# First pass of a two-layer graph network kernel: group comparisons and their sums moved forward, filler matmuls in the first turns, one group check moved ahead of the gathers

## The chip, the cores and the metric

The kernel runs on one core of one Trainium2 chip. The metric is the device time of one execution in microseconds (us). The median of three runs before the change is 1245.95 us. Engines are named as the profile names them: PE (TensorE; PEld is its weight load), DVE (VectorE), ACT (ScalarE), POOL (GpSimd) and SP (SyncE, which only issues DMAs here).

## The reference

Two graph layers run over 100000 nodes with 64 features and 50000 edges, and the edges come sorted by `dst` but not by `src`. Cut to what matters:

```python
h = maximum(layernorm(x), 0)                       # unused by layer 0 but for its shape
s   = segment_sum(edge_attr, src, N)               # layer 0: sum, max, mean of 32 edge features per src node
mx  = where(cnt > 0, segment_max(edge_attr, src, N), 0)
x   = x + relu(concat([s, mx, s / maximum(cnt, 1), u]) @ W1 + b1) @ W2 + b2
h   = maximum(layernorm(x), 0)                     # layer 1
x   = x + relu(segment_sum(h[src], dst, N) @ W.T + b)
```

## The kernel before

The edges are cut into 98 blocks of 512, the nodes into 98 blocks of 1024 rows (8 groups of 128 nodes).

- **Sort (0 to about 171 us).** DVE sorts the edges by `src` in SBUF with compare and exchange steps (lines L931 to L959). Most of them are `tensor_tensor` operations with both inputs in SBUF. Between them PE turns the tile over. `beside_turn` and `between_turns` put other small work between the steps.
- **First pass (from about 186 us).** POOL gathers the edge features of a block into one of eight buffers `xa` with four indirect DMAs (L543). DVE scales them (`scale_attr`, L1073), PE turns them (`turn_attr`), DVE runs two scans over them (`scans`, L1085 and L1087), PE multiplies by W1 (`layer1`), ACT takes the relu (`hidden`, L696), PE multiplies by W2 (`layer2`, L1372), and DVE subtracts a constant row (`less_constant`, L1135) into a record that ACT stores to DRAM. Four to seven turns later windows of records are read back (SP and ACT issue the loads), DVE builds one-hot matrices (`onehots`, L1108), PE expands the records to node rows with them (`expand`, L1384) and DVE adds x (`add_dense`, L1127). In turn n every engine works through its own fixed list: DVE does `scans(n)`, `add_dense(n-7)`, `keys_to_psum(n-5)`, `scale_attr(n+2)`, `onehots(n-5)`, `less_constant(n-1)`. PE does `turn_attr(n+1)`, `expand(n-6)`, `layer2(n-1)`, `layer1(n)`. ACT does `hidden(n-1)`, a record's key and store, then its share of the window loads.
- **Where the windows start.** To load a window the kernel must know at which record each group of 128 nodes begins. `rows_above` compares 800 group numbers with 12 bounds (twelve DVE operations on 128 x 800 f16, L844) and takes the number of edges in each group (L846, L847). `sum_starts` adds these up over the partitions with 24 matmuls of 400 columns (L1309). ACT copies the sums, and `group_starts` on DVE (L852) turns them into `start_row`, for which SP and ACT wait before the first window load (`s_start`). The same is done for `dst` during the sort, where ACT made the comparisons; the result is `near_f`.
- **Checks.** After its last gather of the first pass, POOL checks for `src` and then for `dst` whether the groups fit into the windows (L578 to L587, each operation on one partition with 800 or 784 elements), and presets two one-hot buffers (L573). These share the memory of `above`. ACT sums the checks, and `choice` on DVE (L859) picks the fast path.
- **Second pass (from 713 us).** POOL gathers node rows from the table that the first pass wrote (L562), and a like pipeline runs for `dst`.

In PE's list of the first pass `stream` (L1389) is a matmul of ones whose result nobody reads; `expand` starts with one.

Of the kernel before, what the change touches and what calls it, by code (L numbers as in the profile page):

```python
# [15 lines left out]
P = 128  # L16
# [9 lines left out]
BT = 4  # L26
BLK = BT * P
BLOCKS = -(-E // BLK)
PAIRS = BLOCKS // 2
STEP = 1024  # L30
UNIT = 128
# [38 lines left out]
def valid(n):  # L70

    return 0 <= n < BLOCKS


def build(nc, x, src, dst, edge_attr, u, W1, b1, W2, b2, W, b, src_keys, dst_keys, src_cols, dst_cols, dst_lines, out):
# [5 lines left out]
    with ExitStack() as ctx:  # L81
# [407 lines left out]
        def _(pool):  # L489
# [75 lines left out]

            pool.wait_ge(s_gi, 1)
            for n in range(BLOCKS):
                gather_attr(n)
            for b_ in range(XRING):
                pool.wait_ge(gathered[b_], 16 * BT * len(range(b_, BLOCKS, XRING)))  # L570
            pool.wait_ge(s_base, 2)
            for r, t in enumerate(hot1):
                g.tensor_copy(t[96:P, :, :], ident[96:P, CONST[1]:CONST[1] + 1].unsqueeze(2).to_broadcast([P - 96, PER, UNIT])).then_inc(s_preset1, 1)  # L573
                pool.wait_ge(s_preset1, r + 1)
            pool.wait_ge(s_near, 2)
            pool.wait_ge(s_cast, 2)
            for side, (row, more) in enumerate(((start_f, over), (near_f, over2))):
                link(g.tensor_scalar(room[:, :], row[:, :], float(-ROW), None, ALU.mult))  # L578
                link(g.tensor_tensor(room[:, :], room[:, :], limit[:, :], ALU.add))
                link(g.tensor_scalar(more[:, :], room[:, :], 0.0, None, ALU.is_lt))  # L580
                if side == 1:
                    link(g.tensor_scalar(room[:, :], room[:, :], 0.0, None, ALU.max))
                    link(g.tensor_tensor(room[:, :], limit[:, :], room[:, :], ALU.subtract))
                    link(g.tensor_copy(start_row[1][:, :], room[:, :]))
                link(g.tensor_tensor(room[:, 0:LAST], row[:, 1:LAST + 1], row[:, 0:LAST], ALU.subtract))
                link(g.tensor_scalar(room[:, 0:LAST], room[:, 0:LAST], float(WP), None, ALU.is_gt))
                last = g.tensor_tensor(more[:, 0:LAST], more[:, 0:LAST], room[:, 0:LAST], ALU.add)  # L587
                if side == 0:
                    link(last)
            last.then_inc(s_over, 1)  # L590
            pool.wait_ge(s_fast, 1)
# [36 lines left out]
        def _(act):  # L628
# [30 lines left out]

            act.wait_ge(s_base, 1)  # L660
            for h, row in enumerate(p_s[1]):
# [66 lines left out]
            for n in range(BLOCKS + SRC_WIN):  # L728
# [4 lines left out]
                if n == 3:  # L733
                    act.wait_ge(s_base, 2)
                    for h, row in enumerate(p_s[0]):
                        last = s.copy(start_f[:, 400 * h:400 * (h + 1)], row[0:1, 0:400])
                    last.then_inc(s_near, 1)
# [45 lines left out]
        def _(dve):  # L783
# [56 lines left out]

            def rows_above():

                for k in range(SPAN):
                    v.tensor_scalar(above[:, k, :], group_of[:, :], bound_u[:, k:k + 1], None, ALU.is_gt)  # L844
                dve.wait_ge(s_signs, SPAN * 2)
                link(v.tensor_scalar(less[:, 1:SPAN + 1], signs[:, :], 0.5, COLS / 2, ALU.mult, ALU.add))  # L846
                v.tensor_tensor(in_group[:, :], less[:, 1:SPAN + 1], less[:, 0:SPAN], ALU.subtract).then_inc(s_above, 1)  # L847
# [292 lines left out]
            scale_attr(0)  # L1140
            scale_attr(1)
            for n in range(BLOCKS + SRC_ADD):
                if valid(n):
                    scans(n)
                if valid(n - SRC_ADD):
                    add_dense(0, n - SRC_ADD)
                if valid(n - SRC_HOT):
                    keys_to_psum(0, n - SRC_HOT)
                if valid(n + 2):
                    scale_attr(n + 2)  # L1150
                if valid(n - SRC_HOT):
                    onehots(0, n - SRC_HOT)
                if valid(n - SRC_REC):
                    less_constant(n - SRC_REC)
                if n == 1:
                    rows_above()
                if n == 3:
                    group_starts()
# [129 lines left out]
        def _(pe):  # L1288
# [14 lines left out]

            def sum_starts(side, nth):

                pe.wait_ge(s_above, nth)
                for h, row in enumerate(p_s[side]):
                    for k in range(SPAN):
                        last = mm(row[0:1, 0:400], in_group[:, k:k + 1], above[:, k, 400 * h:400 * (h + 1)],  # L1309
                                  start=k == 0, stop=k == SPAN - 1)  # L1310
                last.then_inc(s_base, 1)
# [10 lines left out]
            def between_turns(t):  # L1322

                if t == 7:
                    sum_starts(1, 1)
                elif t == 5:
# [19 lines left out]
            pe.wait_ge(s_tt[0], 19)  # L1346
            turn_columns(p_u, ha).then_inc(s_pt[0], 1)
            pe.wait_ge(s_tt[0], 20)
            pe.wait_ge(s_gi, 1)
# [42 lines left out]
            for n in range(BLOCKS + SRC_EXP):  # L1392
                if valid(n + 1):
                    turn_attr(n + 1)
                if n == 2:
                    sum_starts(0, 2)
                if valid(n - SRC_EXP):
# [98 lines left out]
```

## Time and profile before

| | us |
|---|---|
| three runs | 1242.65, 1245.95, 1247.1 (median 1245.95) |
| the profiled execution, own time | 1242.97 |
| its span | 1241.2 |
| busy DVE, PE, POOL, ACT | 1021.4, 957.0, 786.6, 282.4 |
| first scan of the first pass | 189.08 |
| last addition of the first pass ends | 709.9 |
| first gather of the second pass | 713.01 |

A row of a timeline gives the start (us), the duration (us), engine, line, operation, output and inputs, shapes, the count of merged instructions, and in brackets how long the engine had been idle before it and what ended that. Times are from the span's start.

### The profile page before, as it was taken

How to read it: one execution, taken by the hardware profiler on the slowest of the kernel's cores; microseconds unless marked ns; L12 is line 12 of the kernel's file. 1: busy time of each engine (PE TensorE's matmuls, PEld its weight loads, DVE VectorE, ACT ScalarE, POOL GpSimd, SP SyncE). 2: the span in 40 equal slices, each digit the busy share in tenths (PEclk: the TensorE clock that was granted, in tenths of full speed). 3: DMA queues.
4: the chain of work that ended last, by engine and by line, in shares of the span. 5: the costliest groups of instructions: out<-in, count | busy, mean ns of one | idle time of the engine just before them, and what ended most of it. 6: DMA issues, size and time to landing. Idle time of an engine off the chain costs nothing.

```text
span 1241.2 us, 20776 instructions
## 1 busy us (share of the span) xinstructions
PE 957.0 (77%) x5818; PEld 758.3 (61%) x5818; DVE 1021.4 (82%) x2718; ACT 282.4 (23%) x685; POOL 786.6 (63%) x836
## 2 busy tenths in 40 slices
PE   0122017999999999999999725898888888978988
PEld 0011004777777777777777514776777677766777
DVE  8888896899999999999999635777677777777785
ACT  1451032222222222222222111111121212111110
POOL 3000037777777777777777577777777777777750
PEclk9996556799999999999999955888898989898989
DMA  2000012788989888888888645686887778787865
GB/s 66 0 0 0 0 32 71 169 229 240 236 232 239 234 234 235 225 231 221 232 228 234 185 136 125 168 230 175 229 211 202 207 197 211 205 221 203 214 172 161
DMA packets 317579, 218.51 MB, mean 176 GB/s; under 512 B 223444, under 2 KB 255156, under 8 KB 317460
## 3 DMA queue, kind: packets, MB, share of 16 engines
q1 hardware_dynamic: 182116, 135.41, 38.8%
q10 hardware_dynamic: 110256, 62.42, 19.3%
q0 software_dynamic: 25088, 19.32, 8.1%
q8 instruction: 47, 0.77, 0.3%
q14 instruction: 72, 0.59, 0.2%
HBM read 137.51 MB, written 79.45 MB: 175 GB/s over the span
## 4 chain that ended last, share of the span: by engine, by line
DVE 48%; POOL 13%; DMA 12%; PE 10%; issue 8%; ACTq 5%; ACT 2%; SPq 0%; DVEq 0%; POOLq 0%
POOL xa L562 13%; DMA xa<-node_table,gi 8%; DVE feats L1087 8%; DVE feats L1085 7%; DVE oneh L1108 6%; DVE dout L1127 4%; DMA win<-records 3%; ACTq L686 3%; DVE rec L1135 2%; DVE kb L933 2%; DVE ka L933 2%; PE p_m L1372 2%; DVE shared L1108 2%; ACT hid L696 2%; DVE ka L934 2%
## 5 line engine op out<-in xcount | busy, mean ns | idle before, releaser
L543 POOL DMA_INDIRECT xa<-in_edge_attr_dram,gi x392 | 374.2, 955 | 232.3 <-issue 119.0
L562 POOL DMA_INDIRECT xa<-node_table,gi x392 | 370.9, 946 | 131.9 <-issue 108.0
L696 ACT ACTIVATE hid<-p_z,bias_z 128x512 f32<-128x512 f32 x98 | 113.7, 1160 | 236.1 <-issue 222.8
L1087 DVE TENSOR_TENSOR_SCAN feats<-c_rows,feats,p_g 32x512 f32<-32x512 f32 x97 | 123.3, 1271 | 1.4
L1413 PE MATMUL p_g<-ident,hn 128*128 128x128 f32 x196 | 46.3, 324 | 100.5 <-DVE hn L1187 100.4
L1085 DVE TENSOR_TENSOR_SCAN feats<-c_rows,feats,p_g 64x512 f32<-64x512 f32 x97 | 122.5, 1263 | 0.5 <-issue 0.5
L749 ACT ACTIVATE sd<-mv,eps_t 128x4 f32<-128x4 f32 x98 | 29.2, 298 | 399.2 <-DVE mv L1178 342.9
L1108 DVE SCALAR_TENSOR_TENSOR oneh<-p_m,node_of 112x1024 f32<-112x1024 f32 x98 | 119.3, 1218 | 0.2
L1372 PE MATMUL p_m<-w_s,hid 128*128 128x64 f32 x784 | 109.2, 283 | 13.0 <-ACT hid L696 12.5
L1108 DVE SCALAR_TENSOR_TENSOR shared<-p_m,node_of 112x1024 f32<-112x1024 f32 x98 | 117.3, 1197 | 2.2 <-PE p_z L1384 0.6
L1389 PE MATMUL p_t<-one 128*128 128x256 f32 (+1 forms) x228 | 113.3, 582 | 0.0
L1384 PEld LDWEIGHTS p_u<-win,oneh 128*128 128x128 f32 x784 | 95.8, 193 | 26.9 <-issue 22.5
L1389 PE MATMUL p_u<-one 128*128 128x512 f32 x230 | 111.2, 568 | 0.0
L1384 PEld LDWEIGHTS p_t<-win,oneh 128*128 128x128 f32 x784 | 95.9, 193 | 24.1 <-issue 23.5
L1365 PE MATMUL p_z<-feats,w_s 96*128 96x512 f32 x196 | 109.4, 640 | 0.4 <-DVE feats L1087 0.4
L1372 PEld LDWEIGHTS p_m<-w_s,hid 128*128 128x128 f32 x784 | 97.4, 195 | 18.7 <-ACT hid L696 16.7
L1173 DVE BATCH_NORM_STATS2 stat<-xa 128x6 f32<-128x64 f32 x392 | 58.7, 212 | 59.9 <-DMA xa<-node_table,gi 59.8
L1098 DVE COPY p_m<-win 112x8 f32<-112x8 f32 x196 | 32.9, 168 | 79.8 <-DMA win<-records 79.7
L1384 PE MATMUL p_u<-win,oneh 128*128 128x64 f32 x784 | 93.8, 273 | 2.8 <-DVE oneh L1108 2.8
L1384 PE MATMUL p_t<-win,oneh 128*128 128x64 f32 x784 | 93.5, 273 | 0.0
L1413 PEld LDWEIGHTS p_g<-ident,hn 128*128 128x128 f32 x196 | 25.4, 159 | 110.0 <-DVE hn L1187 109.7
L1187 DVE SCALAR_TENSOR_TENSOR hn<-xa,mv,p_m 128x64 f32<-128x64 f32 x392 | 83.9, 277 | 3.5
(259 smaller groups left out, 1565.7 us busy)
## 6 DMA issues: line engine op xcount, KB each, us to landing
win<-records SPq DMA_DIRECT2D x980, 28.9 KB
records<-rec ACTq DMA_DIRECT2D x196, 132.0 KB
din<-in_x_dram SPq DMA_DIRECT2D x49, 512.0 KB
node_table<-dout SPq DMA_DIRECT2D x48, 512.0 KB, 3.9
din<-node_table SPq DMA_DIRECT2D x43, 512.0 KB
out_dram<-dout SPq DMA_DIRECT2D x43, 512.0 KB
c_rows<-rows_src ACTq DMA_DIRECT2D x141, 128.0 KB
win<-records ACTq DMA_DIRECT2D x588, 28.9 KB
```

What stands on the lines that cost most here:

```text
L543: g.indirect_dma_start(out=xa[n % XRING][:, t, 0:FE], out_offset=None, in_=edge_attr, in_offset=bass.IndirectOffsetOnAxis(ap=gi[0][:, BT * ...
L562: g.indirect_dma_start(out=xa[k % XRING][:, t, :], out_offset=None, in_=T, in_offset=bass.IndirectOffsetOnAxis(ap=gi[1][:, BT * n + t:BT * ...
L696: s.activation(hid[n % 2][:, :].rearrange("p (t n) -> p n t", n=P), p_z[n % 2][:, :].rearrange("p (n t) -> p n t", t=BT), ACT.Relu, bias=b ...
L1085: v.tensor_tensor_scan(f[0:64, :], c[0:64, at:at + BLK], p_g[n % 2][0:64, :], first[0:64], ALU.mult, ALU.add)
L1087: v.tensor_tensor_scan(f[64:96, :], c[64:96, at:at + BLK], p_g[n % 2][0:32, :], first[64:96], ALU.min, ALU.max).then_inc(feats_ok, 1)
L1108: v.scalar_tensor_tensor(hots[side][m % HRING][0:WP, :, :], key_at(k).unsqueeze(2).to_broadcast([WP, PER, UNIT]), -float(STEP * m), node_o ...
L1187: last = v.scalar_tensor_tensor(hn[n % 2][:, t, :], xa[(BLOCKS + n) % XRING][:, t, :], mv[n % 2][:, t, 0:1], up[:, t:t + 1].to_broadcast([ ...
L1365: mm(p_z[n % 2][:, :], w1_s[:, :], feats[n % 2][:, :], start=True, stop=True).then_inc(z_ok, 1)
L1372: last = mm(p_m[0][:, D * t:D * (t + 1)], hid[n % 2][:, P * t:P * (t + 1)], w2_s[:, :], start=True, stop=True)
L1384: last = mm(to[:, D * s:D * (s + 1)], hots[side][m % HRING][:, s, :], win[k % WRING][:, s, 0:D], start=True, stop=True)
L1389: mm(bank[:, 0:width], one[:, :], one[:, :].unsqueeze(1).to_broadcast([P, width // P, P]), start=True, stop=True)
L1413: last = tr(p_g[n % 2][:, P * h:P * (h + 1)], hn[n % 2][:, 2 * h:2 * h + 2, :].rearrange("p t d -> p (t d)"), ident[:, :])
```

## The change

Four edits, all in the first pass and the sort:

1. `rows_above` is split. The first six comparisons stand ahead of turn 0, the other six and the group counts (`rows_in_group`) in turn 0, behind `scale_attr(2)` and ahead of the second scan. Before, all of it stood in turn 1.
2. `sum_starts` works on one half (12 matmuls). For `src` the halves stand in turns 1 and 2 of PE's list, before `layer2`; before, both stood in turn 2. For `dst` both halves still stand at the same place of the sort.
3. Filler matmuls of ones: two into the two `p_z` banks between the turn of `ha` and the turns of `sorted_in` and `spare`, and a `stream` into `p_z` in each of turns 0, 3, 4 and 5.
4. POOL checks the `dst` groups once `near_f` is there, ahead of the first gather of the first pass. Only the check for `src` stays behind the last gather, and the presets of `hot1` come behind that.

```diff
-            for side, (row, more) in enumerate(((start_f, over), (near_f, over2))):
+            def check_groups(side, row, more):
...
+            pool.wait_ge(s_near, 1)
+            pool.wait_ge(s_cast, 2)
+            check_groups(1, near_f, over2)
             pool.wait_ge(s_gi, 1)
             for n in range(BLOCKS):
                 gather_attr(n)
             for b_ in range(XRING):
                 pool.wait_ge(gathered[b_], 16 * BT * len(range(b_, BLOCKS, XRING)))
-            pool.wait_ge(s_base, 2)
-            for r, t in enumerate(hot1):
...
+            pool.wait_ge(s_near, 2)
+            check_groups(0, start_f, over)
+            pool.wait_ge(s_base, 4)
+            for r, t in enumerate(hot1):
...
-                    act.wait_ge(s_base, 2)
+                    act.wait_ge(s_base, 4)
...
             scale_attr(1)
+            rows_above(0, SPAN // 2)
             for n in range(BLOCKS + SRC_ADD):
...
                     onehots(0, n - SRC_HOT)
+                if n == 0:
+                    rows_above(SPAN // 2, SPAN)
+                    rows_in_group()
                 if valid(n - SRC_REC):
                     less_constant(n - SRC_REC)
-                if n == 1:
-                    rows_above()
...
+            def sum_starts(side, h):
+
+                pe.wait_ge(s_above, 2 - side)
+                for k in range(SPAN):
+                    last = mm(p_s[side][h][0:1, 0:400], in_group[:, k:k + 1], above[:, k, 400 * h:400 * (h + 1)],
+                              start=k == 0, stop=k == SPAN - 1)
                 last.then_inc(s_base, 1)
...
                 if t == 7:
+                    sum_starts(1, 0)
                     sum_starts(1, 1)
...
             turn_columns(p_u, ha).then_inc(s_pt[0], 1)
+            for z in p_z:
+                mm(z[:, :], one[:, :], one[:, :].unsqueeze(1).to_broadcast([P, BT, P]), start=True, stop=True)
...
-                if n == 2:
-                    sum_starts(0, 2)
+                if n in (1, 2):
+                    sum_starts(0, n - 1)
+                elif n < SRC_EXP:
+                    stream(p_z[n % 2], BLK)
```

## Rows read from the trace of the kernel before

**Rows 1.** The page: shares of the chain that ended last.

```profile
DVE 48%; POOL 13%; DMA 12%; PE 10%; issue 8%; ACTq 5%; ACT 2%; SPq 0%; DVEq 0%; POOLq 0%
```

**Rows 2.** Timeline of DVE in the first turns.

```profile
189.08 1.27 DVE L1085 TENSOR_TENSOR_SCAN feats<-c_rows,carry,p_g 64x512 f32<-64x512 f32 x1 [2.34 <-PE p_g L1360]
...
197.05 0.42 DVE L1135 TENSOR_TENSOR rec<-p_m,c_neg 128x256 f32<-128x256 f32 x1 [2.30 <-PE p_m L1372]
197.39 4.25 DVE L844 TENSOR_SCALAR shared<-group_of,bound_u 128x800 f16<-128x800 f16 x12
...
209.11 0.43 DVE L1135 TENSOR_TENSOR rec<-p_m,c_neg 128x256 f32<-128x256 f32 x1 [4.37 <-PE p_m L1372]
...
212.70 0.97 DVE L852 SCALAR_TENSOR_TENSOR start_row<-start_f,limit 1x800 int32<-1x800 f32 x1
```

**Rows 3.** Waits, 184 to 240 us: us in total, times, longest.

```profile
DVE rec L1135 <- PE p_m L1372: 12.8, 5, 4.4
```

**Rows 4.** Timeline of PE in the first turns.

```profile
186.20 1.13 PE L1301 MATMUL p_t<-ident,ka 128*128 128x128 f32 x4 [2.50 <-DVE ka L1051]
...
201.98 4.03 PE L1309 MATMUL p_t<-shared,in_group 128*1 128x400 f16 x12 [2.30 <-DVE in_group L847]
205.84 2.19 PE L1309 MATMUL p_u<-shared,in_group 128*1 128x400 f16 x12
...
222.23 1.97 PE L1372 MATMUL p_m<-w_s,hid 128*128 128x64 f32 x8 [0.93 <-ACT hid L696]
...
226.66 1.91 PE L1389 MATMUL p_t<-one 128*128 128x512 f32 x2
...
235.55 1.06 PE L1372 MATMUL p_m<-w_s,hid 128*128 128x64 f32 x8
```

**Rows 5.** Busy times by stretch; PEclk is the granted clock.

```profile
200.00:205.00 5.00, 3.02 (x10) 1.18 (x11) 4.66 (x10) 0.03 (x1) 3.99 (x4) 0.50 0.32 85
...
220.00:225.00 5.00, 4.07 (x15) 2.78 (x14) 3.91 (x7) 1.33 (x2) 3.78 (x5) 0.50 0.77 199
...
230.00:235.00 5.00, 5.00 (x36) 3.96 (x35) 3.15 (x4) 1.01 (x2) 3.78 (x5) 1.00 0.62 169
```

**Rows 6.** Timelines of POOL and DVE: a middle block's and the last block's gathers.

```profile
473.00 0.95 POOL L543 DMA_INDIRECT xa<-in_edge_attr_dram,gi  x1 [0.31 <-issue]
...
482.37 0.28 DVE L1073 TENSOR_TENSOR xa<-xa,share 128x128 f32<-128x128 f32 x1
...
663.55 0.95 POOL L543 DMA_INDIRECT xa<-in_edge_attr_dram,gi  x1 [0.30 <-issue]
668.56 2.13 POOL L573 COPY shared<-ident 32x1024 f32<-32x1024 f32 x2 [4.07 <-issue]
```

**Rows 7.** The chain: start, us, what; a gather's way from issue to landing.

```profile
726.89 2.42 DMA xa<-node_table,gi
```

**Rows 8.** Timelines of ACT and POOL around the new place of the check.

```profile
95.62 0.87 ACT L662 COPY near_f<-p_m 1x400 f32<-1x400 f32 x2 [17.16 <-PE p_m L1309]
...
170.97 1.18 POOL L543 DMA_INDIRECT xa<-in_edge_attr_dram,gi  x1 [112.97 <-ACT gi L716]
```

**Rows 9.** Timeline of POOL: the first and last of nine operations of the check that moves.

```profile
683.10 2.20 POOL L578 TENSOR_SCALAR room<-near_f 1x800 f32<-1x800 f32 x1
...
698.59 1.84 POOL L587 TENSOR_TENSOR over<-over,room 1x784 f32<-1x784 f32 x1
```

**Rows 10.** Timelines of POOL and DVE where both read SBUF.

```profile
675.05 2.21 POOL L580 TENSOR_SCALAR over<-room 1x800 f32<-1x800 f32 x1
675.52 0.53 DVE L1073 TENSOR_TENSOR xa<-xa,share 128x128 f32<-128x128 f32 x1
...
212.78 1.72 POOL L543 DMA_INDIRECT xa<-in_edge_attr_dram,gi  x1 [0.30 <-issue]
```

**Rows 11.** Groups of DVE instructions, 96.5 to 113.5 us: busy us, mean ns.

```profile
L933 DVE TENSOR_TENSOR ka<-kb 128x256 f32<-128x256 f32 x8 | 3.4, 426 | 0.3
```

**Rows 12.** Timeline of DVE at the end of the first pass.

```profile
709.85 0.15 DVE L859 TENSOR_REDUCE wrong<-wrong 128x1 f32<-128x6 f32 x1
```

More of the change, by code:

```diff
@@ L564, in gather_x @@
                         in_offset=bass.IndirectOffsetOnAxis(ap=gi[1][:, BT * n + t:BT * n + t + 1], axis=0)).then_inc(gathered[k % XRING], 16)
[L566 to L570, printed above, removed]
-            pool.wait_ge(s_base, 2)
-            for r, t in enumerate(hot1):
[L573 to L576, printed above, removed]
-            for side, (row, more) in enumerate(((start_f, over), (near_f, over2))):
+            def check_groups(side, row, more):
                 link(g.tensor_scalar(room[:, :], row[:, :], float(-ROW), None, ALU.mult))
@@ L587, in _ @@
                 last = g.tensor_tensor(more[:, 0:LAST], more[:, 0:LAST], room[:, 0:LAST], ALU.add)
-                if side == 0:
+                if side == 1:
                     link(last)
-            last.then_inc(s_over, 1)
+                else:
+                    last.then_inc(s_over, 1)
+            pool.wait_ge(s_near, 1)
+            pool.wait_ge(s_cast, 2)
+            check_groups(1, near_f, over2)
+            pool.wait_ge(s_gi, 1)
+            for n in range(BLOCKS):
+                gather_attr(n)
+            for b_ in range(XRING):
+                pool.wait_ge(gathered[b_], 16 * BT * len(range(b_, BLOCKS, XRING)))
+            pool.wait_ge(s_near, 2)
+            check_groups(0, start_f, over)
+            pool.wait_ge(s_base, 4)
+            for r, t in enumerate(hot1):
+                g.tensor_copy(t[96:P, :, :], ident[96:P, CONST[1]:CONST[1] + 1].unsqueeze(2).to_broadcast([P - 96, PER, UNIT])).then_inc(s_preset1, 1)
+                pool.wait_ge(s_preset1, r + 1)
             pool.wait_ge(s_fast, 1)
@@ L658, in _ @@
             act.wait_ge(s_cast, 2)
-            act.wait_ge(s_base, 1)
+            act.wait_ge(s_base, 2)
             for h, row in enumerate(p_s[1]):
@@ L839, in bounds, with rows_above, rows_in_group @@
                 v.tensor_scalar(bound[:, :], bound_u[:, :], float(UNIT), UNIT / 2 - 0.5, ALU.mult, ALU.add).then_inc(s_bound, 1)
-            def rows_above():
-                for k in range(SPAN):
+            def rows_above(first, end):
+                for k in range(first, end):
                     v.tensor_scalar(above[:, k, :], group_of[:, :], bound_u[:, k:k + 1], None, ALU.is_gt)
+            def rows_in_group():
                 dve.wait_ge(s_signs, SPAN * 2)
@@ L1302, in turn_columns @@
                 return last
[L1304 to L1310, printed above, removed]
+            def sum_starts(side, h):
[3 more added lines that the diff above has]
+                              start=k == 0, stop=k == SPAN - 1)
                 last.then_inc(s_base, 1)
```

## Prediction

> **What bounds the kernel now.** I first read the page's shares of the chain that ended last: DVE carries about half of it [rows 1]. Then I read the timelines of DVE, PE, ACT and POOL from 160 to 250 us, turn by turn, since every edit but one lies there. The reader is to see three things. First, a turn from the eighth on is one unbroken row of DVE work, while in turns 1, 2, 4, 5 and 6 DVE waits for PE at `less_constant`; these five waits come to 12.8 us [rows 3], the longest (4.37 us) right behind the sums of `sum_starts`, which hold PE from 201.98 us to 207.97 us [rows 2, 4]. Second, PE runs at the lower of its two levels in most of these turns: the granted clock is 0.50 (1.2 GHz) from 200 to 205 and from 220 to 225 us, after stretches with gaps in PE's work, and 1.00 (2.4 GHz) from 230 us, after turns filled by the stream and the expansion [rows 5]. Third, POOL issues a gather about every 1.25 us without a pause, four to a block, so (663.55 - 473.00) / 38 = 5.01 us a block from block 59 to block 97; DVE scales the same two blocks at 482.37 and 675.52 us, 5.08 us a block with its small stalls [rows 6, 10]. The two go at nearly the same pace. Whatever the first turns give back, DVE then runs closer behind the gathers. After the last block the rest of the pass and the second pass follow at fixed distances.
>
> **The change, part by part.**
>
> *The comparisons.* Twelve take 4.25 us, 0.354 us each [rows 2]. The first six (2.1 us) fall into the 2.34 us in which DVE waits for PE before the first scan [rows 2]: cost nothing; without that cover 2.1 us. The other six and the two small operations for the counts (about 0.3 us) stand ahead of the second scan: it moves from about 191.9 us (two scans and a scaling behind the first) to about 194.4 us. DVE waited 2.30 us at the end of that turn anyway [rows 2], so most of this is hidden too, and 4.5 us leave turn 1.
>
> *The sums.* Twelve matmuls took 4.03 us at the low level and about 2.1 us after the clock rose [rows 4]. The counts are there at about 194.4 us. I take 2.0 us for a half: the first ends at 196.4, `layer2(0)` (1.0 us, [rows 4]) at 197.4, `less_constant(0)` at 197.8: the third scan starts at 197.9 us, where now it stands behind the comparisons and counts (197.39 + 4.25 + 0.2 = 201.9 us, [rows 2]): 4.0 us earlier. The second half ends at about 200.9 and `layer2(1)` at 201.9, where before the record waited until 209.11 us [rows 2]: the fourth scan, right behind the record, starts at 202.3 instead of 209.4 us, 7.1 us earlier. ACT copies the sums at about 204 us, `start_row` follows some 7 us before 212.70 us [rows 2], and so do SP's and ACT's first window loads and everything that ACT has queued behind its wait for them (`hidden(3)` above all).
>
> *The fillers.* Ones of 512 columns take about 1.7 us at the low level (1.91 us is the pair of records, overlapping what follows) and 0.9 us at the high one [rows 4]. Two of them, 3.4 us, go into a gap of 2.50 us before the turns at 186.20 us [rows 4]: up to 0.9 us late, nothing if the clock rises meanwhile. What they are to give is the clock. `layer2` takes 1.97 us at the low level and 1.06 us at the high one [rows 4]. In turns 4 to 6 DVE waits 12.8 - 2.3 - 4.4 = 6.1 us for PE [rows 2, 3]. With a high clock I count 0.9 us less in each of the first two, and 2.5 us in the third, where a stream, an expansion and `layer2` stand in a row: 4.3 us. The eighth scan would start 7.1 + 4.3 = 11.4 us earlier. If the clock gives nothing it is still 7.1 us.
>
> *What the gathers let through.* Here the gain is cut. Block 59's last gather is issued at 473.00 us and its scaling runs at 482.37 us [rows 6], 9.37 us later, the shortest distance from block 5 on that I found. How long a gather takes to land is not shown for these. From below, 2.42 us from issue in a quiet stretch [rows 7]; from above, the last one, issued at 663.55 us, is there by 668.56 us, when POOL comes through its wait for all of them [rows 6]: at most 5.0 us. DMA is busier in this pass than in the quiet stretch, so I take 3.9 us, a little nearer to the upper end. That leaves DVE 9.4 - 3.9 = 5.5 us to gain (4.4 to 6.9). The start-up gain of 7 to 11 us exceeds this, so 5.5 us reach the end of the pass, and DVE shows waits for gathers in their place. The stalls of later turns stay as they are.
>
> *The check that moves.* At its old place it costs nothing: POOL ends at 700.4 us and DVE asks for the verdict at 709.85 us [rows 9, 12], 9.4 us of cover for ACT's two sums, and the check for `src` with the presets behind it is done earlier than both checks were. At its new place POOL is idle until 170.97 us and `near_f` is there at 96.5 us [rows 8], so its nine operations, 17.3 us from first to last [rows 9], never delay the first gather by themselves; the cover is some 57 us. But they read SBUF beside a sort whose every step is on the path. Between 96.5 and 113.5 us DVE has 30 exchange operations with both inputs in SBUF (this group of 8 and three more of 8, 7 and 7) [rows 11]. The trace has one meeting of that kind: with POOL's operation of 675.05 us under way, the scaling of block 97 took 0.53 us instead of 0.28 us [rows 6, 10]. So the price lies between nothing, 9 x 0.25 = 2.3 us (one meeting for each of POOL's operations), 30 x 0.25 = 7.5 us (each exchange is held up) and 17.3 us (DVE stands still while POOL works). The one row shows a delay much shorter than POOL's 2.21 us, so I take 2.3 us and keep 0 and 17.3 as ends. This delay would move the sort's end, the first gather and all that follows.
>
> The Trainium skill, page "SBUF — State Buffer", section "Who interferes with whom", says that a DVE instruction with two SBUF inputs and a GpSimd instruction that reads SBUF share one read interface, and that the later one "fully blocks" until the first has finished. In one direction the trace agrees: a gather issue took 1.72 us instead of 0.95 us beside the DVE operation of 212.70 us, which has two SBUF inputs [rows 2, 10]. In the other it does not: the scaling began 0.47 us into POOL's operation and ended 1.2 us before it did [rows 10]. By the page the change would cost about 17 us less 5.5 us, by my row 2.3 us less 5.5 us.
>
> *Sum.* 2.3 - 5.5 = -3.2 us. The profiled execution's own time is 1242.97 us (1.8 us around the span of 1241.2 us), which gives 1239.8 us. That execution lies 3.0 us below the median of the three runs; the mean of all four is 1244.7 us, and I set the prediction against it: 1241.5 us. A measurement of this kernel can tell about 0.5%, 6.2 us.
>
> **The rivals.**
>
> - *The check is free.* For it: POOL's operations touch a single partition, and the one delayed DVE operation may be chance. Then -5.5 us (-4.4 to -6.9): 1239.2 us.
> - *Each exchange is held up.* 7.5 - 5.5 = +2.0 us: 1246.7 us. For it: the one meeting in the trace did cost 0.25 us. Against: it was one operation after DVE work that has one SBUF input, not a dense row.
> - *DVE stands still while POOL works* (the other side). Place: 96.5 to 114 us, the steps of the sort. Price 17.3 us less the 2.5 us in which DVE waits for PE anyway, so 15 to 17 us: net +9 to +12 us, about 1255 us. It decides from a hold of about 1.3 us for each of the nine operations on (11.7 us less 5.5 us is 6.2 us). Against it stands the 0.53 us row. It is the way in which the rule of the Trainium skill's page "SBUF — State Buffer", section "Who interferes with whom", would act here.
> - *The clock stays low and the fillers stand in the way.* At the low level a filler is 1.7 us and a half of the sums 4.0 us, both ahead of `layer2`: by the same reckoning `less_constant(0)` comes at 202.2 and `less_constant(2)` near 217.3 us instead of just before 212.70 us [rows 2], some 5 us late, +7 us with the check, 1252 us. Against it: the clock rose while the sums ran and again after the turn with the first stream [rows 4, 5].
>
> **How the numbers follow.** Partial hold, -3.2 us: 0.47. Check free: 0.27. Each exchange held up: 0.12. DVE stands still: 0.10. Low clock: 0.04. Faster by over 0.5%: half of the free check's case (its range ends at -6.9 us) and a tenth of the likeliest, 0.19. Slower: the standstill, most of the low clock and a little of the third case, 0.15. Within 0.5%: 0.66. The range goes from 1244.7 - 6.9 less about 2 us for the spread of the runs, 1236 us, to 1251 us, which leaves out the standstill and most of the low clock. The likeliest case alone: 1238 to 1245 us.
>
> **What the profile after would show.** The twelve comparisons ahead of 195 us, in two groups; `start_row` at about 206 us plus the delay of the sort; the granted clock at 1.00 from about 190 us and without a fall before the steady turns; no wait of 2 us or more at `less_constant` in turns 3 to 6. DVE waits for gathers (at the scaling) in turns 5 to 60, which are not there now. POOL's nine operations from 96.6 us, exchanges beside them of more than 0.43 us, and the first gather later than 170.97 us by the price of the check. The distance from the first gather to the first one of the second pass, now 542.0 us, shorter by 4.4 to 6.9 us. I am wrong if that distance shrinks by much more (then gathers do not hold DVE), by nothing (then the first turns gain nothing or a later stall grows), or if the first gather moves by over 5 us.

## The result and the profile after

The changed kernel took 1250.8 us (median of 20 runs), the kernel before 1246.7 us (20 runs beside it on the same chip): a ratio of 1.0042, 95% interval 1.0023 to 1.0061, some 5 us slower. Medians here and below are taken over all runs, ratios from the means of the undisturbed ones, so the two can differ a little. The prediction was 1241.5 us. The time lies in its range by 0.2 us, but the direction is wrong. The profiled execution took 1247.21 us with a span of 1245.4 us, 4.2 us more than before.

The timeline of POOL shows the nine operations of the check at their new place:

```profile
97.32 2.22 POOL L568 TENSOR_SCALAR room<-near_f 1x800 f32<-1x800 f32 x1 [39.35 <-ACT near_f L668]
99.62 2.10 POOL L569 TENSOR_TENSOR room<-room,limit 1x800 f32<-1x800 f32 x1
101.81 2.28 POOL L570 TENSOR_SCALAR over<-room 1x800 f32<-1x800 f32 x1
...
113.61 1.82 POOL L577 TENSOR_TENSOR over<-over,room 1x784 f32<-1x784 f32 x1
```

The timeline of DVE has this beside it:

```profile
99.92 2.09 DVE L943 TENSOR_TENSOR kb<-ka 128x256 f32<-128x256 f32 x1
...
104.50 1.07 DVE L943 TENSOR_TENSOR ka<-kb 128x256 f32<-128x256 f32 x1
...
113.64 2.09 DVE L943 TENSOR_TENSOR kb<-ka 128x256 f32<-128x256 f32 x1
```

An exchange took 426 ns before [rows 11]. The exchanges that are held delay the sort, so not 30 but 18 exchanges with both inputs in SBUF now run beside the check. Eight of these take 0.85 to 2.09 us, 7.4 us more than 0.42 us each; the other ten take 0.42 us as before. The exchange of 99.92 us ends 0.29 us after POOL's operation of 99.62 us, that of 113.64 us ends 0.30 us after POOL's of 113.61 us. The sort ends later by this much; the indices (timeline of ACT) were ready at 169.59 us before:

```profile
176.89 1.07 ACT L722 CAST gi<-p_t 128x512 int32<-128x512 f32 x1 [66.04 <-PE p_t L1312]
```

The first turns, on DVE:

```profile
196.38 1.27 DVE L1094 TENSOR_TENSOR_SCAN feats<-c_rows,carry,p_g 64x512 f32<-64x512 f32 x1 [0.35 <-DMA c_rows<-rows_src]
...
209.57 0.43 DVE L1144 TENSOR_TENSOR rec<-p_m,c_neg 128x256 f32<-128x256 f32 x1 [1.29 <-PE p_m L1385]
...
213.18 0.97 DVE L861 SCALAR_TENSOR_TENSOR start_row<-start_f,limit 1x800 int32<-1x800 f32 x1
...
223.99 0.35 DVE L1082 TENSOR_TENSOR xa<-xa,share 128x128 f32<-128x128 f32 x1 [2.06 <-DMA xa<-in_edge_attr_dram,gi]
...
233.38 0.42 DVE L1144 TENSOR_TENSOR rec<-p_m,c_neg 128x256 f32<-128x256 f32 x1 [2.92 <-PE p_m L1385]
```

The first scan begins 7.3 us later than in [rows 2], the first gather 7.9 us later (178.91 instead of 170.97 us), and `start_row` is only 0.5 us later. The waits at `less_constant` from 184 to 240 us, to be read against [rows 3], and one new wait for a gather:

```profile
DVE rec L1144 <- PE p_m L1385: 6.9, 5, 2.9
DVE xa L1082 <- DMA xa<-in_edge_attr_dram,gi: 2.1, 1, 2.1
```

PE in the same stretch (to be read against [rows 4]), and the granted clock (the third number from the end, to be read against [rows 5]):

```profile
201.80 2.19 PE L1319 MATMUL p_t<-shared,in_group 128*1 128x400 f16 x12 [1.24 <-DVE in_group L856]
206.31 2.19 PE L1319 MATMUL p_u<-shared,in_group 128*1 128x400 f16 x12
...
217.15 1.64 PE L1385 MATMUL p_m<-w_s,hid 128*128 128x64 f32 x8 [2.14 <-ACT hid L702]
...
223.83 1.97 PE L1385 MATMUL p_m<-w_s,hid 128*128 128x64 f32 x8 [0.66 <-ACT hid L702]
```

```profile
190.00:195.00 5.00, 5.00 (x18) 3.05 (x19) 4.88 (x13) 1.09 (x1) 3.78 (x5) 0.64 0.46 139
195.00:200.00 5.00, 2.98 (x14) 1.33 (x12) 4.61 (x9) 1.98 (x2) 3.78 (x5) 1.00 0.38 94
...
215.00:220.00 5.00, 2.86 (x11) 2.06 (x11) 3.19 (x5) 1.33 (x2) 3.78 (x4) 0.75 0.72 142
220.00:225.00 5.00, 4.34 (x13) 2.25 (x11) 2.89 (x5) 1.13 (x1) 3.77 (x4) 0.50 0.51 94
225.00:230.00 5.00, 5.00 (x13) 2.66 (x13) 4.56 (x7) 1.34 (x2) 3.77 (x4) 0.50 0.90 215
```

The clock does go up early, at 195 us, and both halves of the sums run at the high level. Then ACT comes late with `hid`, PE stands for 2.14 us, and from there to about 230 us the clock is back at 0.50 (1.2 GHz).

The rest of the way in four distances (us, from the two profiled executions):

| stretch | before | after |
|---|---|---|
| start to the indices of the sort | 169.6 | 176.9 |
| indices to the eighth scan | 62.6 | 56.8 |
| eighth to last scan (90 turns) | 450.3 | 451.9 |
| last scan to the first gather of the second pass | 30.6 | 32.2 |
| from there to the end | 528.2 | 527.6 |

So the check takes 7.3 us, the first turns gain 5.8 us, 3.2 us of it are given back before the second pass begins, and the rest is 0.5 us shorter: +4.2 us.

### The profile page after: what moved, and what is told of

Same layout as the page of the kernel before. It is cut to its first block, busy times and chain, and to the rows that moved or that the text cites. A ratio compares the mean times of both kernels' runs of the same rounds, so it can differ in the third digit from the quotient of the medians.

```text
span 1245.4 us, 20802 instructions
## 1 busy us (share of the span) xinstructions
PE 959.2 (77%) x5830; PEld 758.3 (61%) x5830; DVE 1029.1 (83%) x2718; ACT 281.8 (23%) x685; POOL 784.2 (63%) x836
## 4 chain that ended last, share of the span: by engine, by line
DVE 48%; POOL 13%; PE 12%; DMA 12%; issue 8%; ACTq 5%; ACT 2%; DVEq 0%; SPq 0%; POOLq 0%
POOL xa L562 13%; DMA xa<-node_table,gi 9%; DVE feats L1096 7%; DVE feats L1094 7%; DVE oneh L1117 6%; DVE dout L1136 4%; ACTq L692 3%; PE p_m L1385 2%; DMA win<-records 2%; DVE shared L1117 2%; DVE kb L942 2%; DVE ka L942 2%; DVE kb L943 2%; DVE rec L1144 2%; DVE ka L943 2%
## 5 line engine op out<-in xcount | busy, mean ns | idle before, releaser
L702 ACT ACTIVATE hid<-p_z,bias_z 128x512 f32<-128x512 f32 x98 | 113.5, 1158 | 236.0 <-issue 222.6
```

The source lines that it names most:

```text
L702: s.activation(hid[n % 2][:, :].rearrange("p (t n) -> p n t", n=P), p_z[n % 2][:, :].rearrange("p (n t) -> p n t", t=BT), ACT.Relu, bias=b ...
```

## The experiments

Ratios are to the kernel before, which ran in the same calls on the same chip.

**Where the check stands.** Theory A: POOL's operations that read SBUF hold the exchanges, some 7 us for nine. Rivals: any POOL work there would do it, or the 5 us come from the other three edits. `check_only` is the kernel before with edit 4 alone, `check_back` the changed kernel with both checks behind the gathers (the presets still come last), `write_only` is `check_back` with twelve POOL operations that read nothing at the early place, and `check_twice` makes the early check twice.

```diff
# check_back
-            check_groups(1, near_f, over2)
             pool.wait_ge(s_gi, 1)
...
             pool.wait_ge(s_near, 2)
+            pool.wait_ge(s_cast, 2)
+            check_groups(1, near_f, over2)
             check_groups(0, start_f, over)
# write_only: check_back, and ahead of pool.wait_ge(s_gi, 1)
+            for _ in range(12):
+                link(g.iota(limit_i[:, :], ...))
# check_twice: the changed kernel
             check_groups(1, near_f, over2)
+            check_groups(1, near_f, over2)
```

> The kernel before with the fourth edit alone: the check of the dst groups stands ahead of the first gather, nothing else is changed. Theory A (POOL's operations that read SBUF hold up DVE's exchanges with two SBUF inputs, and the whole rest follows the sort): the profile after showed 7.3 us for it (gather indices cast at 176.89 instead of 169.59 us), so this kernel is slower by about 7 us, ratio 1.006, and its gather indices come at about 177 us. Theory B (the check costs little and the other three edits make the kernel slower): ratio 1.000 to 1.002.

> The changed kernel with the check of the dst groups back behind the last gather; the other three edits stay. Theory A: the gather indices come at 169.6 us again, the distance from the first gather to the first one of the second pass stays some 3 us shorter than before (538.9 against 542.0 us in the two profiles), so faster than before by about 3 us, ratio 0.9975. Theory B (the other edits cost by themselves): ratio above 1.002.

> check_back with twelve iotas of 800 numbers on one partition (about 1.4 us each, 17 us in all) at the place where the changed kernel had the check: POOL is as busy there but only writes SBUF. They write limit_i, which has been read by then; the result is not changed. Theory A (it is POOL's reads against DVE's second input): no exchange takes more than 0.45 us, the sort ends when it does in check_back, ratio to before about 0.9975. Rival A2 (any POOL work beside the sort holds DVE up): 5 to 8 us slower than check_back, ratio about 1.003.

> The changed kernel with the early check of the dst groups made twice in a row (18 instead of 9 operations, the same values). Theory A: the second nine cost about as much as the first, 7 us more than the changed kernel: gather indices at about 184 us, ratio to before about 1.010. Theory B: no more than 1 us above the changed kernel, ratio 1.004 to 1.005.

| | median us | ratio, 95% interval | indices ready at | exchanges held |
|---|---|---|---|---|
| check_only | 1257.1 | 1.0078 (1.0039 to 1.0118) | 176.3 | 7, 6.0 us |
| check_back | 1243.3 | 0.9984 (0.9949 to 1.0019) | 169.4 | none |
| write_only | 1244.4 | 0.9985 (0.9951 to 1.0019) | 169.8 | none |
| check_twice | 1262.8 | 1.0103 (1.0047 to 1.0160) | 184.8 | 15, 14.4 us |

In `check_only` and in `check_twice` one more DVE operation with two SBUF inputs (`added_rows`, 0.28 us before) takes 1.5 us longer. The timelines of POOL and DVE in `write_only`, and of ACT in `check_twice`:

```profile
96.94 17.05 POOL L586 IOTA limit_i<- 1x800 int32 x12 [38.98 <-ACT near_f L671]
102.61 1.20 DVE L839 TENSOR_SCALAR part_f<-c_bc,ident 128x64 f32<-128x64 f32 x1
```

```profile
184.77 1.08 ACT L723 CAST gi<-p_t 128x512 int32<-128x512 f32 x1 [72.43 <-PE p_t L1313]
```

17.05 us of POOL work that only writes beside the same stretch of the sort hold no exchange. One other DVE operation, `part_f`, takes 1.20 us instead of 0.25 us; DVE then has to wait for PE anyway, and the indices come 0.2 us later than in the kernel before. One check moves the indices by 7.3 us, a second one by 7.9 us more. Theory A stands, and with the check back the kernel is level with the one before. The time of `check_only` is higher than edit 4's 7 us explains; its interval reaches down to 1.0039 (4.9 us). Its profiled execution (1264.75 us, one of its longest) also has 14.3 us of waits at `less_constant` between 240 and 690 us, against 3.9 us in the kernel before, though its first turns are no shorter.

**Whether the gathers cap the gain.** With three gathers for a block instead of four (a quarter of the edge features is left out), the last gather is issued at 639.9 us instead of 663.55 us, and from block 5 on no block's last gather is issued less than 10.9 us before its scaling, so none holds DVE. The waits for a block's gathers count three instead of four, and POOL fills the gather buffers with zeros early in the sort. Theory: the gathers cut the gain, so `three_back` keeps all of it. Rival: something else does.

```diff
-                for t in range(BT):
+                for t in range(BT - 1):
                     if t == 0 and n >= XRING:
```

> The kernel before with three gathers of edge features a block instead of four in the first pass (a quarter of the edges' features is left out and zeros stand for them; POOL fills the gather buffers with zeros early in the sort). POOL then needs some 3.8 us a block against DVE's 4.92 us, and less is transferred. It is the baseline for the next run. Theory C (what the first turns give back is lost later because gathers and the other transfers leave DVE and ACT no room): the stalled turns of over 5.2 us from turn 7 on, ten in the profile before, mostly go, and the kernel gets faster by 5 us or more, ratio 0.996 or less. Rival D (the stalls come from ACT's and SP's own loads and stores alone): ratio 0.999 to 1.001 and the stalls stay.

> check_back (edits 1 to 3, the check at its old place) with three gathers a block instead of four (the same part is left out as in three_before). Theory C: the 6.7 us that the first turns gained (from the gather indices to the eighth scan 55.9 instead of 62.6 us) now reach the end: 5 to 7 us below three_before. Rival D: it is 1 to 3 us below three_before, as check_back is to before.

`three_before` took 1249.6 us, 1.0032 (1.0006 to 1.0058), `three_back` 1246.4 us, 1.0021 (0.9995 to 1.0046): 3.1 us apart in the medians (1.8 us in the means, give or take 3.7), where the eighth scan is 7.0 us earlier (225.1 against 232.1 us). Most of the gain is given back without any help of the gathers. My cap falls. The 1.0032 of `three_before` lies above both of my expectations for it (the interval reaches down to 1.0006), and I have no cause for that.

**Which of the edits help.** `no_fillers` has the comparisons and the sums in halves alone (edits 1 and 2; the presets still come behind the checks), `fillers_only` the ones alone (edit 3). Theory: the ones are worth 4 us at the eighth scan and less at the end. Rival: nothing at all.

```diff
# no_fillers: check_back without
-            for z in p_z:
-                mm(z[:, :], one[:, :], one[:, :].unsqueeze(1).to_broadcast([P, BT, P]), start=True, stop=True)
...
-                elif n < SRC_EXP:
-                    stream(p_z[n % 2], BLK)
```

> check_back without the filler matmuls: edits 1 and 2 alone (comparisons and sums moved). By the prediction's reckoning they are worth 7.1 us up to the fourth scan, less what the lower clock makes of it (a half of the sums 4.0 instead of 2.1 us, layer2 1.97 instead of 1.06 us): the eighth scan some 3 to 5 us after the gather indices earlier than before (62.6 us), and little of it at the end: ratio 0.998 to 1.000. If the fillers are what brings the gain, the eighth scan comes at 61 us or later.

> The kernel before with the third edit alone (fillers in turns 0, 3, 4 and 5 and ahead of the last turns of the sort). With the clock up from 190 us the sums take 4.3 instead of 6.0 us and layer2 half: the eighth scan 2 to 4 us earlier (59 to 61 us after the gather indices), at the end ratio 0.998 to 1.000. If the fillers stand in the way instead: 63 us or more, ratio above 1.001.

> The kernel with the comparisons ahead of the second scan and the sums in halves alone, once more. In the earlier call it was at 0.9975 [0.9952, 0.9997] of before. If that is its own worth, it is again 2 to 4 us below before; if it was chance, within 1 us.

> The same two edits and the ones in the first turns, check back behind the gathers, once more, on the same chip as no_fillers_2. If the ones bring the last 1 to 2 us that they bring at scan 7, it is 1 to 2 us below no_fillers_2; if they do nothing for the end, within 1 us of it, both 1 to 3 us below before; if they cost something later, 1 to 2 us above it.

| | median us | ratio, 95% interval | eighth scan | waits at `less_constant`, 240 to 690 us |
|---|---|---|---|---|
| no_fillers | 1241.6 | 0.9975 (0.9952 to 0.9997) | 226.4 | 6.2 us, 8 |
| no_fillers_2 | 1237.1 | 0.9959 (0.9940 to 0.9979) | 226.8 | 9.1 us, 15 |
| check_back_2 | 1241.5 | 0.9995 (0.9967 to 1.0022) | 224.4 | 9.2 us, 12 |
| fillers_only | 1244.9 | 1.0001 (0.9977 to 1.0024) | 230.2 | 13.9 us, 15 |

Edits 1 and 2 alone beat the kernel before and the changed one, twice: 0.25% and 0.41% below the kernel before, 3 to 5 us. That is less than the 0.5% that I named as what a measurement tells, but both intervals lie below 1. The ones bring the eighth scan 1 to 2.4 us forward and show no gain at the end; with them the kernel was 1.7 us (`check_back`, from another call) and 4.4 us (`check_back_2`, same call and chip) slower in the median than without. The intervals overlap, so I say no more than that no gain by the ones is shown at the end.

**What gives the gain back.** The places are in the profile. In the trace of `check_back`, timelines of ACT, DVE and PE around the worst turn:

```profile
553.31 2.90 ACTq L691 DMA_DIRECT2D win<-records  x2
556.25 1.13 ACT L701 ACTIVATE hid<-p_z,bias_z 128x512 f32<-128x512 f32 x1 [4.85 <-issue]
...
560.99 0.82 ACTq L691 DMA_DIRECT2D win<-records  x2
```

```profile
559.44 0.42 DVE L1143 TENSOR_TENSOR rec<-p_m,c_neg 128x256 f32<-128x256 f32 x1 [3.13 <-PE p_m L1384]
```

```profile
557.43 1.97 PE L1384 MATMUL p_m<-w_s,hid 128*128 128x64 f32 x8 [2.32 <-ACT hid L701]
```

ACT needs 2.90 us to issue two window loads where 0.82 us is usual; its relu is late by that, PE stands for 2.32 us, the clock falls (0.84 from 550 to 560 us, 0.82 from 560 to 570 us), `layer2` takes 1.97 us instead of 1.06 us [rows 4], and DVE waits 3.13 us: (2.90 - 0.82) + (1.97 - 1.06) = 3.0 us. First rival for the slow issues: the load on the DMA engines. `nodense_before` and `nodense_back` leave out the loads of x in the first pass (but for two pairs of blocks, from which they go on adding).

```diff
             def load_dense(side, k, table):
+                if side == 0 and k >= 2:
+                    return
...
-                    dve.wait_ge(d_in[side][pair_ % 2], 16 * (pair_ // 2 + 1))
+                    dve.wait_ge(d_in[side][pair_ % 2], 16 * (pair_ // 2 + 1) if side else 16)
```

> The kernel before, but its first pass loads the dense x tiles only for the first two pairs of blocks and goes on computing from those (so the output no longer follows from the whole x); the gathers, records and second pass stay. What is asked: what makes the stalled turns of the first pass (turns over 5.2 us) that gave the earlier start back. If it is the load on the DMA engines (their share was about 0.9 there, with ACT's window-load issues at 1.6 to 2.9 us instead of 0.8), most stalled turns go, turns 7 to 97 take 443 to 447 us instead of 450 to 460, and the kernel is 5 to 12 us faster than before. If the stalls come from something else (the chain of records, ACT's own queue), they stay and the time is within 3 us of before.

> The changed kernel with the dst check back behind the gathers, and the same dense loads left out. If the load on the DMA engines gives back the earlier start, this one is 5 to 7 us below nodense_before, as much as scan 7 is earlier in it. If the start-up gain is lost to something else, the two stay within 3 us, as check_back (1243.3) and before (1244.3) did.

`nodense_before` took 1245.3 us, 1.0018 (0.9997 to 1.0040), `nodense_back` 1242.9 us, 0.9980 (0.9953 to 1.0007): 2.4 us apart. The stalls stayed (10 and 15 turns over 5.2 us between 240 and 690 us, against 10 in the kernel before and 13 in `check_back`), although DMA's share fell from 0.90 to 0.75 (250 to 450 us). So it isn't the traffic of x. The next theory took the window loads themselves: ACT issues two of a block's eight, SP six. `sp8` leaves all eight to SP and takes the call out of ACT's list, `sp7` leaves one to ACT (7 in the same place).

```diff
-SP_LOADS = (6, 4)
+SP_LOADS = (8, 4)
...
-                if valid(n - SRC_WIN):
-                    upper_windows(0, n - SRC_WIN)
```

> The kernel before with all 8 window loads of a first-pass block issued by SP (6 before) and none by ACT. If ACT's slow issues ahead of its relu make the stalled turns, none of those with a late hid stays, and turns 7 to 97 take 443 to 447 us where before took 450.3: 2 to 7 us faster. Rival: SP, whose issues for a block then take 8 x 0.45 + 0.42 = 4.0 us of a 4.9 us turn (an estimate from its 2.7 us for six and 0.42 us for a store), comes late itself, windows land late, and the kernel is slower by as much.

> The same for the changed kernel with the dst check back behind the gathers. If ACT's issues gave the start-up gain back, it is 5 to 7 us below sp8_before and turns 7 to 97 are as long in both; if something else does, the two stay within 3 us of each other.

> Comparisons ahead of the second scan and sums in halves alone, with 7 window loads on SP and 1 on ACT. An issue of one load by ACT is half as long, so a slow one (1.45 us at most) hides behind the 2.2 us in which ACT waits anyway: 1 to 4 us below the same version with six and two (1237.1 to 1241.6), if ACT's issues matter; the same within 1 us, if not.

> The same with all 8 on SP. If ACT's issues are all that stalls, it equals sp7_no_fillers or is 1 us below it; if SP's 4.0 us of issues for a turn make windows late, it is slower than sp7_no_fillers.

| | median us | ratio, 95% interval |
|---|---|---|
| sp8_before | 1271.9 | 1.0199 (1.0165 to 1.0234) |
| sp8_back | 1265.5 | 1.0150 (1.0117 to 1.0184) |
| sp8_no_fillers | 1267.4 | 1.0158 (1.0120 to 1.0195) |
| sp7_no_fillers | 1279.8 | 1.0274 (1.0237 to 1.0312) |

DVE's waits from 240 to 690 us, first in the kernel before, then in `sp8_before` (us in total, times, longest):

```profile
DVE rec L1135 <- PE p_m L1372: 3.9, 9, 0.9
```

```profile
DVE p_m L1096 <- DMA win<-records: 25.2, 30, 2.6
```

The waits behind ACT are gone, and a larger one is there: windows land late. That was the rival. `sp7_no_fillers`, which I had expected 1 to 4 us below the split of six and two, came out the slowest, with 32.6 us of such waits; why one load on ACT is worse than none I can't say. But `sp8_before` and `sp8_back` are now 6.4 us apart, where the eighth scan is 9.0 us earlier (222.0 against 231.0 us): here most of the start-up gain stays. The other direction, three loads on ACT:

```diff
-SP_LOADS = (6, 4)
+SP_LOADS = (5, 4)
```

> The kernel before with 5 window loads of a first-pass block on SP and 3 on ACT (6 and 2 before). If ACT's issues ahead of its relu make the stalled turns, three of them take 1.2 us in a quiet turn, still inside the 2.2 to 2.5 us in which ACT waits anyway, and 2.3 to 4 us in a slow one: DVE's waits for PE at less_constant between 240 and 690 us grow from 3.9 us to 10 us or more, and the kernel is 3 to 10 us slower. If the stalls came from the windows' landing behind SP's other transfers, this kernel is equal or up to 3 us faster.

> The same split for the kernel with the comparisons ahead of the second scan and the sums in halves alone. By ACT's issues: no gain over sp5_before of more than 3 us, since an earlier start meets more of them. By the windows' landing: 4 to 5 us below before, or better.

`sp5_before` took 1348.4 us, 1.0832 (1.0798 to 1.0865), `sp5_no_fillers` 1337.1 us, 1.0737 (1.0694 to 1.0780). I had expected 3 to 10 us and got 102. The reason shows when one puts ACT's timelines of the kernel before and of `sp5_before` side by side:

```profile
404.71 0.20 ACT L702 COPY rec<-rn 128x4 f32<-128x4 f32 x1 [1.19 <-PE p_m L1372]
405.30 0.39 ACTq L713 DMA_DIRECT2D records<-rec  x1
406.32 0.81 ACTq L686 DMA_DIRECT2D win<-records  x2
407.17 1.16 ACT L696 ACTIVATE hid<-p_z,bias_z 128x512 f32<-128x512 f32 x1 [2.26 <-issue]
...
409.55 0.20 ACT L702 COPY rec<-rn 128x4 f32<-128x4 f32 x1 [1.22 <-PE p_m L1372]
```

```profile
402.50 0.20 ACT L702 COPY rec<-rn 128x4 f32<-128x4 f32 x1 [2.12 <-PE p_m L1372]
403.01 0.43 ACTq L713 DMA_DIRECT2D records<-rec  x1
404.76 1.30 ACTq L686 DMA_DIRECT2D win<-records  x3
406.11 1.16 ACT L696 ACTIVATE hid<-p_z,bias_z 128x512 f32<-128x512 f32 x1 [3.41 <-issue]
...
408.46 0.20 ACT L702 COPY rec<-rn 128x4 f32<-128x4 f32 x1 [1.19 <-PE p_m L1372]
```

ACT is in a closed loop: key of a record, its store, the window loads, the relu, then `layer2` on PE, which releases the next key. The store waits for DVE's `less_constant` too, so DVE's pace is in the distance of two keys, and that distance doesn't measure the loop: it is 409.55 - 404.71 = 4.84 us here, and 4.84 us as well in `sp8_before`, where ACT issues no window load:

```profile
400.69 0.20 ACT L702 COPY rec<-rn 128x4 f32<-128x4 f32 x1 [2.59 <-PE p_m L1370]
405.53 0.20 ACT L702 COPY rec<-rn 128x4 f32<-128x4 f32 x1 [2.50 <-PE p_m L1370]
```

What measures it is the way from the start of a `less_constant` to the end of the next `layer2`. Its median between 240 and 690 us is 3.23 us in `sp8_before`, 4.80 us in the kernel before and 5.92 us in `sp5_before`. DVE's own turn without a wait takes 4.92 us (its scalings in the changed kernel at 472.54, 477.47 and 482.39 us), so in the kernel before some 0.1 us lie between the two. The third load lengthens the loop by 1.1 us (in the medians 0.4 us more between the store and the loads, 0.5 us more for the loads), and DVE waits the difference in nearly every turn:

```profile
DVE rec L1135 <- PE p_m L1372: 78.7, 73, 2.8
```

## Why the prediction was wrong

In the two profiled executions the sum of -3.2 us became +4.2 us: 5.0 us of the difference lie in the price of the check (7.3 instead of 2.3 us), 2.4 us in the gain that reaches the end (3.1 instead of 5.5 us).

**The price of the check** is the step that turned the sign. I wrote "The one row shows a delay much shorter than POOL's 2.21 us, so I take 2.3 us". It measured 7.3 us, shown by the indices (176.89 against 169.59 us), by `check_back` and by `check_twice`. The mechanism was right and the size was three times too small: I had one meeting of a single scaling, and priced nine like it. In the dense row of the sort an exchange is held for up to 1.7 us. With 7.3 us in my sum it would have read 7.3 - 5.5 = +1.8 us. My third rival has this total (7.5 us, 1246.7 us), but not this form: not each of 30 exchanges is held by 0.25 us, but eight of the 18 beside the check by 0.4 to 1.7 us. The rule of the Trainium skill's page "SBUF — State Buffer", section "Who interferes with whom", is nearer to the traces than my one row: five of the eight end 0.28 to 0.30 us after an operation of POOL's ended, as if they had waited for it. It doesn't hold for every pair: ten exchanges went on beside POOL's operations in 0.42 us, eight of them begun in the middle of one, and the total is 7.4 us, not the 15 to 17 us that I worked out from it. For two SBUF inputs it also counts only reads, and `write_only` agrees: 17.05 us of writes held no exchange.

**The comparisons and the sums** were nearly right. The eighth scan was to be 7.1 us nearer to the sort's end without help of the clock; with edits 1 and 2 alone it is 62.6 - 56.8 = 5.8 us nearer (`no_fillers`; 5.2 us in `no_fillers_2`).

**The fillers** were to give 4.3 us more. From the indices to the eighth scan they gave 0.9 us in `check_back` (55.9 against 56.8 us), 2.5 us in `check_back_2` (54.9 against 57.4 us), 3.4 us in `write_only` (53.4 against 56.8 us), and in the changed kernel nothing (56.8 us). I had the clock "without a fall before the steady turns"; it fell at about 217 us, behind a PE gap of 2.14 us that no one of the fillers stands in, for it comes from ACT: its wait for `start_row` stands ahead of `hidden(3)`. I named that wait, and gave it no price.

**The gathers as the cap** ("so 5.5 us reach the end of the pass") is a wrong mechanism, and its number was too high as well. The first gather to the first one of the second pass was to shrink by 4.4 to 6.9 us; it shrank by 3.1 us, from 542.0 to 538.9 us. DVE does run closer behind the gathers, as I said (6.4 us instead of 9.37 us at the closest behind turn 8: the gather of 359.00 us, the scaling of 365.40 us), but the waits for gathers "in turns 5 to 60" are one, 2.1 us at 223.99 us, and none later (1.8 us in two waits in `no_fillers`, 1.3 us in three in `check_back_2`, none in `check_back`, 3.2 us in three in `write_only`). With the gathers out of the way only 3.1 of 7.0 us stayed. I read the chain and the distances, and didn't ask what else runs at the same pace as DVE: ACT's loop, some 0.1 us short of DVE's turn. "The stalls of later turns stay as they are" was the failed sentence. The waits at `less_constant` between 240 and 690 us were 3.9 us in the kernel before, 6.0 us in the changed one, 6.2 to 12.3 us in `no_fillers`, `no_fillers_2`, `check_back_2` and `check_back`. Those right behind a pair of window loads that ACT took over 1.2 us to issue are 3.0 of 3.9 us in the kernel before, 4.9 of 6.0 us in the changed one, 7.5 of 12.3 us in `check_back` and 3.6 of 9.1 us in `no_fillers_2`. The others mostly follow a longer gap ahead of the loads (about 1.1 instead of 0.63 us), or PE is late in the turn behind a stall.

**What stays open.** That slow issues of ACT's make stalls is shown by the timelines and by the sums above. Why more waiting comes of them after an earlier start is not. They don't become more frequent: pairs that took over 1.4 us are five in the kernel before and four to eight in each other profile with six loads on SP. And `check_only`, whose first turns are no shorter, has 14.3 us of waits, so one profile of each kernel doesn't even show that the earlier start is what brings them. My theory said that ACT's issues give the gain back; then the `sp5` pair should have lain within 3 us, and it lay 11.3 us apart, more than the 6.6 us by which its eighth scan is earlier. The `sp8` pair, with no issue on ACT, lay 6.4 us apart, as the theory has it. Where a slower loop sets the pace, most of the start-up gain or all of it stays; at the balance of the kernel before, 3 to 5 of 5 to 6 us stay with edits 1 and 2, and little with the ones. Between 240 and 690 us, in stretches of 10 us, the granted clock fell below 0.99 in no or one place in five of the six profiles without the ones, but in four places in the sixth (`check_only`), and in one to four places in each of eight with them (six loads on SP in all of these). Whether the ones cause that, or chance does, would need more profiles than I have. What made an issue of two loads take 2.9 us was not found; it was not the traffic of x.

## What to carry to other kernels

Work that is moved into an engine's idle time is priced by what runs beside it: where POOL reads SBUF beside a dense row of DVE operations with two SBUF inputs on the critical path, one meeting in the trace gives no mean, and each operation of POOL's can be a hold (here 7.3 us for nine). Before you forecast that a gain at the start reaches the end, measure each closed loop of the steady stage, DMA issues included: an engine at 23% busy had a loop of 4.80 us in a turn of 4.92 us, and one more DMA issue in it cost 8%. Take the loop from the point where the busiest engine lets it go: the distance of two equal events of it is the turn's, whichever engine sets that. Try the parts of a change alone: two of the four edits here make a kernel 3 to 5 us faster, which the other two hide.

## What the hardware showed that I had not expected

- Of the eight held exchanges seven begin within 0.33 us after an operation of POOL's began (99.92 after 99.62, 104.50 after 104.17, 113.64 after 113.61 us); exchanges that begin later in such an operation pass, but for one. Three end while POOL's operation is still under way, after 0.95 to 1.07 us.
- A third window load per turn cost ACT 0.4 us ahead of its first load (in the median 1.06 us between the store's end and the loads, 0.63 us before; 1.32 us in the turn shown), besides 0.5 us for its own issue. The steps between, in which the window's start is read from SBUF into a register, are no row of the timeline; the gap is.
- Moving one or two window loads of a block from ACT to SP made the kernel 1.5 to 2.7% slower: 25 us of waits for windows in `sp8_before`, as a rule every second or every fourth turn. One load left on ACT (1279.8 us) was worse than none (1267.4 us).
- POOL's writes held one DVE operation, no exchange: `part_f`, which reads `c_bc` and a column of `ident`, took 1.20 instead of 0.25 us in `write_only`. POOL's iota began 0.04 us after it, and it ended 0.05 us after the iota.
